# A dilated 7x7 convolution in front of a token attention: its sum over column taps taken from a pass through DRAM into TensorE, and the stages behind it moved by four slots

## The reference

```python
x0 = x
x = _gn(x)                                     # each channel of each image to mean 0, variance 1
y = conv_general_dilated(x, conv_w, strides 1, padding 15, rhs_dilation 5)   # 7x7, one output channel
y = batch norm of y
imp = sigmoid(gelu(y))                         # (B, 1, 110, 110)
xs = x * imp
idx = sort(top_k(imp, 192))                    # 192 pixels of each image
tokens = xs at idx + positions at idx          # (B, 192, 32)
t1 = layernorm(tokens + attention(tokens))     # 8 heads of 4
t2 = layernorm(t1 + feed forward of t1)
out = x0 + (x with t2 written at idx)
```

## Time and profile before

| | us |
|---|---|
| median of 3 runs | 1159.2 |
| lowest, highest | 1155.85, 1162.91 |
| span of the profiled execution | 1225.6 |
| TensorE busy in it | 971.3 (79%) |
| VectorE busy | 835.0 (68%) |
| ScalarE busy | 774.3 (63%) |
| GpSimd busy | 631.8 (52%) |
| mean granted TensorE clock | 0.884 |

### The profile page before, as it was taken

One profiled execution on the slowest core, in us unless ns is written; L12 is line 12 of the kernel. 1 busy time (PEld: TensorE's weight loads), 2 busy tenths in 40 slices (PEclk: granted clock), 3 DMA queues, 4 the chain that ended last, 5 costly groups with the idle time before them and its releaser, 6 DMA issues.

```text
span 1225.6 us, 21628 instructions
## 1 busy us (share of the span) xinstructions
PE 971.3 (79%) x6440; PEld 762.4 (62%) x6440; DVE 835.0 (68%) x2114; ACT 774.3 (63%) x1899; POOL 631.8 (52%) x851
## 2 busy tenths in 40 slices
PE   3986865689888988898889889986786786488676
PEld 2765643577667766776678667865664565366544
DVE  5345776488558967896879677976694676455644
ACT  2545644486547786877688768875866575267543
POOL 4333316632665368546854576557516655562352
PEclk8998988799879999999899999998987589699855
DMA  9998977555566989898989888965453555436778
GB/s 244 314 264 227 272 210 180 146 159 157 133 156 184 266 217 237 236 291 208 233 238 274 228 238 227 265 187 143 132 169 98 132 154 151 123 98 195 212 221 269
DMA packets 176252, 247.82 MB, mean 202 GB/s; under 512 B 65512, under 2 KB 71912, under 8 KB 176136
## 3 DMA queue, kind: packets, MB, share of 16 engines
q1 hardware_dynamic: 167944, 244.03, 71.9%
q0 software_dynamic: 8192, 2.40, 1.5%
HBM read 124.53 MB, written 121.80 MB: 201 GB/s over the span
## 4 chain that ended last, share of the span: by engine, by line
PE 38%; DVE 20%; ACT 12%; issue 9%; DMA 9%; another core or an unknown queue 6%; POOL 5%; SPq 1%; ACTq 0%; DVEq 0%; POOLq 0%
PE cv L527 10%; PE sc L646 7%; PE pp L659 4%; PE xb L511 4%; PE tr L561 3%; DVE res L1350 3%; ACT wgt L843 3%; PE ib L574 2%; ACT pr L872 2%; PE ms L675 2%; DMA table<-xt 2%; DMA X<-in_x 2%; DVE stats L1126 2%; DMA tok_pos<-in_pos,idx 2%
## 5 line engine op out<-in xcount | busy, mean ns | idle before, releaser
L527 PE MATMUL cv<-X,w_conv 128*128 128x330 f32 (+1 forms) x1024 | 302.2, 422 | 11.6 <-issue 5.9
L527 PEld LDWEIGHTS cv<-X,w_conv 128*128 128x128 f32 x1024 | 193.3, 203 | 45.9 <-issue 12.1
L843 ACT ACTIVATE wgt<-ib,eps_col,mom 128x440 f32<-128x440 f32 (+1 forms) x256 | 177.6, 701 | 46.3 <-DVE res L1350 22.0
L1145 DVE TENSOR_SCALAR_CACHE_REDUCE junk<-flat,th 128x379 bf16<-128x379 f32 x200 | 120.6, 603 | 115.3 <-ACT th L829 89.3
L511 PE MATMUL xb<-cst,X 128*110 128x128 f32 x900 | 153.7, 297 | 48.8 <-ACT xt L809 28.3
L646 PE MATMUL sc<-k_b,qm 128*128 128x192 f32 x768 | 172.2, 353 | 16.2 <-DVE pixf L1245 7.3
L1046 POOL TENSOR_SCALAR res<-res,mom 128x440 f32<-128x440 f32 (+1 forms) x152 | 96.0, 634 | 171.0 <-DVE res L1350 169.3
L1350 DVE SCALAR_TENSOR_TENSOR res<-tr,mom,wgt 128x440 f32<-128x440 f32 (+1 forms) x192 | 122.2, 641 | 71.4 <-PE tr L561 31.0
L809 ACT COPY xt<-xb 110x512 f32<-110x512 f32 x225 | 131.6, 585 | 58.9 <-PE xb L511 30.7
L872 ACT ACTIVATE pr<-sc,least 128x192 f32<-128x192 f32 x384 | 137.1, 415 | 31.0 <-DVE least L1314 18.6
L659 PE MATMUL pp<-cst,pr 128*96 128x128 f32 x768 | 122.5, 284 | 33.6 <-ACT pt L883 25.4
(11 more groups left out here) (170 smaller groups left out, 1534.2 us busy)
## 6 DMA issues: line engine op xcount, KB each, us to landing
table<-xt SPq DMA_DIRECT2D x240, 224.0 KB
rt<-table SPq DMA_DIRECT2D x240, 224.0 KB
out<-res SPq DMA_DIRECT2D x320, 137.5 KB
X<-in_x SPq DMA_DIRECT2D x64, 412.5 KB, 6.4
X<-in_x SPq DMA_DIRECT2D x64, 343.8 KB, 6.5
conv_rows<-cvr SPq DMA_DIRECT2D x64, 188.0 KB
y<-conv_rows SPq DMA_DIRECT2D x64, 165.4 KB
out<-res SPq DMA_DIRECT2D x64, 68.8 KB
```

Of the source, the lines that this page charges most:

```text
L527: last = mm(cv[:, 0:CUT[half]], w_conv[:, 4 * q + z], X[:, m % XI, at0:at0 + CUT[half]], start=z == 0, stop=z == 3)
L843: last = A(wgt[:, n % 2, at0:at0 + w], ib[:, at0:at0 + w], ACT.Identity, scale=mom[:, NB * g + b, 2:3], bias=eps_col[:, 1:2])
```

## The change

The convolution is turned around. Now `X` is the stationary operand and the weights are what streams: for each of the five rows inside a block (`r`), and each of six row-block groups (`k`), `conv_rows` loads 110 pixels of a row (four row blocks by 32 channels on the partitions) and streams 49, 70, 70, 70, 63 or 35 columns of weights, which are column tap by output row block. The result lies with pixel columns on 110 partitions. ACT copies it into `taps` in two parts (three rows, 462 columns, then two rows, 308 columns; `rows_copy`), each written 110 elements apart. `conv_taps` then multiplies each of the seven taps with a shifted identity (`shift`), so that the shift by 5 pixels and the sum over taps happen in PSUM, and ACT copies 110x110 into `yy` (`taps_copy`). `cvr`, `y7`, `conv_rows` in DRAM, `round_out`, `taps_in` and `importance_sum` are gone. `w_conv` shrinks from 1024 to 105 columns, `cst` grows by 140. Image `b` has its rows in slots BASE[b] to BASE[b]+4 and its taps in BASE[b]+5. All stages from GELU on have numbers smaller by 4; LOAD, INTO, MOMENTS and NORMAL stay.

```diff
-    OUT_T, CUT = 11, (3 * H, 2 * H)
+    KG, WIDE = 6, H // DIL * KS
+    SPLIT_R = 3
-        TAPS, SUM = (10, 17, 25, 31), (15, 20, 28, 32)
-        GELU, IMP_OUT, FLAT, SEARCH, IMP_IN = 33, 35, 38, 40, 58
...
-        SCATTER, BACK, IMPB = 122, 127, (123, 127, 135, 142)
+        TAPS = 5
+        GELU, IMP_OUT, FLAT, SEARCH, IMP_IN = 29, 31, 34, 36, 54
...
+        SCATTER, BACK, IMPB = 118, 123, (119, 123, 131, 138)
...
+        rows_at = {BASE[b] + r: (b, r) for b in range(NB) for r in range(DIL)}
+        taps_at = {BASE[b] + TAPS: b for b in range(NB)}
...
-                eng.wait_ge(conv_ok, upto(conv_ok, (m - XI) // NB, 4 * ((m - XI) % NB) + 3))
+                eng.wait_ge(conv_ok, upto(conv_ok, (m - XI) // NB, 2 * ((m - XI) % NB) + 1))
...
-            def round_out(g, r):
...
-            def taps_in(g, b):
...
-            def conv_part(g, r, first, last_z):
...
+            def conv_rows(g, b, r):
+                m = NB * g + b
+                if r == 0 and m:
+                    pe.wait_ge(y_cp, upto(y_cp, 0, m - 1))
+                if r == SPLIT_R:
+                    pe.wait_ge(cv_cp, upto(cv_cp, g, 2 * b))
+                at0 = WIDE * (r % SPLIT_R)
+                for k in range(KG):
+                    pe.wait_ge(xn_ok, upto(xn_ok, g, 3 * b + k // 2))
+                    low = 4 * k - KS // 2
+                    lo, hi = max(0, low), min(H // DIL, low + KS + 3)
+                    w0 = KS * (KS + 3) if k == KG - 1 else KS * (lo - low)
+                    row = H * (DIL * k + r)
+                    last = mm(cv[0:H, at0 + KS * lo:at0 + KS * hi], X[:, m % XI, row:row + H], w_conv[:, w0:w0 + KS * (hi - lo)],
+                              start=k == 0, stop=k == KG - 1, skip_group_check=True)
+                if r in (SPLIT_R - 1, DIL - 1):
                     last.then_inc(conv_ok, 1)
+            def conv_taps(g, b):
+                pe.wait_ge(cv_cp, upto(cv_cp, g, 2 * b + 1))
+                for k in range(KS):
+                    last = mm(cv[0:H, 0:H], taps[:, k], shift[:, DIL * k:DIL * k + H], start=k == 0, stop=k == KS - 1)
+                last.then_inc(y_ok, 1)
...
-            def round_copy(g, r):
...
+            def rows_copy(g, b, part):
+                act.wait_ge(conv_ok, upto(conv_ok, g, 2 * b + part))
+                lo, hi = ((0, SPLIT_R), (SPLIT_R, DIL))[part]
+                nc.scalar.copy(taps[:].rearrange("p k (q r) -> p r q k", r=DIL)[:, lo:hi],
+                               cv[0:H, 0:WIDE * (hi - lo)].rearrange("p (r q k) -> p r q k", r=hi - lo, k=KS)).then_inc(cv_cp, 1)
+            def taps_copy(g, b):
+                act.wait_ge(y_ok, upto(y_ok, g, b))
+                if g:
+                    act.wait_ge(imp_ok, upto(imp_ok, g - 1))
+                nc.scalar.copy(yy[:, b], cv[0:H, 0:H]).then_inc(y_cp, 1)
...
-            def importance_sum(g, b):
-                dve.wait_ge(y7_in[b], upto(y7_in[b], g))
-                v.reduce_sum(yy[:, b], y7[:, b].rearrange("p k j -> p j k"), AX).then_inc(y_ok, 1)
```

More of the change, by code:

```diff
@@ L83, in preact_conv_token_attention @@
         bones_f = take(128, 128)
+        shift = take(H, H + (KS - 1) * DIL)
         blk = sb("blk", [128, 128], fp16)
@@ L192, in preact_conv_token_attention @@
         xn_ok = raised("xn_ok", 3 * NB)
[L193 to L196, removed]
+        conv_ok = raised("conv_ok", 2 * NB)
+        cv_cp = raised("cv_cp", 2 * NB)
         y_ok = raised("y_ok", NB)
+        y_cp = raised("y_cp", NB)
         gelu_ok = raised("gelu_ok")
@@ L465, in _ @@
                     back_in(g, n + RT)
-                for g, n in at(s, 1, U):
-                    if n in round_end and round_end[n] % 2:
-                        round_out(g, round_end[n])
-                for b in range(NB):
-                    for g, n in at(s, TAPS[b]):
-                        taps_in(g, b)
                 for g, n in at(s, PARTS_OUT):
@@ L750, in _ @@
                 for g, n in at(s, 0, U):
-                    for part in rounds[n][0:1]:
-                        conv_part(g, part[0], part[1], part[2])
+                    if n in rows_at:
+                        conv_rows(g, *rows_at[n])
+                    if n in taps_at:
+                        conv_taps(g, taps_at[n])
                 for g, n in at(s, SCORES, U):
@@ L757, in _ @@
                     thresholds(g)
-                for g, n in at(s, 0, U):
-                    for part in rounds[n][1:2]:
-                        conv_part(g, part[0], part[1], part[2])
                 for g, n in at(s, RANKS):
@@ L1416, in _ @@
                     find_ranks(g)
-                for b in range(NB):
-                    for g, n in at(s, SUM[b]):
-                        importance_sum(g, b)
                 for g, n in at(s, GELU + 1):
@@ L1492, in positions, with conv_bands @@
     return pe
-def conv_bands(w, rows=11):
+def conv_bands(w):
     import numpy as np
     C, n, _ = w.shape
-    out = np.zeros((4 * C, 8, 128), np.float32)
-    for z in range(8):
-        half, at = z // 4, z // 4 * 2 + z % 4
-        for s in range(4):
-            low = 4 * at + s - rows * half - 3
-            for t in range(max(0, low), min(rows - 1, low + n - 1) + 1):
-                if 4 * at + s < 2 * rows:
-                    out[C * s:C * s + C, z, t:n * rows:rows] = w[:, :, t - low]
-    return out.reshape(4 * C, 8 * 128)
+    wide = n + 3
+    out = np.zeros((4, C, wide, n), np.float32)
+    for s in range(4):
+        for d in range(s, s + n):
+            out[s, :, d] = w[:, s - d + n - 1]
+    end = out[:, :, 0:wide // 2].copy()
+    end[2:] = 0
+    return np.concatenate([out.reshape(4 * C, -1), end.reshape(4 * C, -1)], axis=1)
 def packed_weights(a, C, NB, H, half):
```

98 lines of the change are left out of this document (26 added, 72 removed).

## The result

The changed kernel takes 1211.7 us (median of 4, 1208.7 to 1216.0) against 1158.8 (1155.9 to 1162.9): ratio 1.044 [1.041, 1.048]. The forecast was 1130 with a range of 1102 to 1161; it was wrong in sign.

What follows compares the result with a forecast made beforehand. The prediction took transfers to bound the first stretch and TensorE, with DVE and DMA close behind, the overlapped one. Its terms summed to -31 us on the profiled 1225.6, scaled -29, giving 1130 us, range 1102 to 1161.

Steps and rivals of the forecast that it cites:

- "If all, -12. I take 0": TensorE's convolution work, 237 to 225 us at full clock: between +35 and -12 us depending on the empty slots, taken as 0.
- products of 145 ns: Sign of being wrong: TensorE's new products taking 145 ns, as if load and stream didn't overlap, instead of about 95.
- "GpSimd: I take +4": Normalising on GpSimd: an image's first row now needs all three normalised parts, before one; +4 us.
- second rival: Slower: POOL's parts late behind gathers and scatters, 2.7 us twice in 8 groups, 43 us; 1167 us, chance 0.1.
- "-17" at the group's end: End of a group's convolution: DVE's tap wait and sum before Gelu replaced by taps and a copy; -17 us.
- "-6" for the other sums: The other 24 tap sums, 36.5 us off DVE: between 0 and 36 us, taken as -6.
- "-5" for transfers: Convolution data no longer written and read back, 22.6 MB: -5 us in the first stretch.
- "-5" for the slots: The end comes four slots sooner: between -14 and 0 us, taken as -5.
- "-4" for SP: SP's standing still at the convolution, 26.5 + 22.5 us, goes: -4 us.
- "+3" for strided copies: ScalarE's new copies write elements 440 bytes apart at 1.7 times the time per element: 0 to 15 us, taken as +3.
- first rival: Gain stays off the path: TensorE's unevenness, sums beside other work, strided copies; +7, 1166 us, half as bad 1148; chance 0.2.

Runs made afterwards that it cites:

- e_wide: Changed kernel with every row product streaming 105 columns instead of 35 to 70, importance not the reference's: 1180.6 us, 1.018 of the kernel before.
- e_norm: Changed kernel with an image's three normalising parts one slot sooner: 1187.2 us, 1.023 of the kernel before.
- e_sum1: Kernel before with each VectorE sum reading one tap of seven, importance not the reference's: 1154.1 us, 0.996 of the kernel before.
- e_pad_norm: Changed kernel streaming 105 columns per row product, surplus ones over zeros, and normalising one slot sooner: 1164.3 us, 1.004 of the kernel before.
- e_late4: Changed kernel with the stages from Gelu on put back by four slots to their old numbers: 1208.8 us, 1.041 of the kernel before.
- e_contig: Changed kernel with ScalarE writing `taps` in adjacent elements, tap products loading at 28-byte steps, five DMAs for `ge` instead of one: 1213.7 us, 1.048.
- e_even_dve2: e_dve2 with products of images 0 to 2 dealt 6, 6, 6, 4, 4, 4 over six slots, taps in the seventh: 1156.2 us, 0.996.
- e_dve2: e_pad_norm with image 2 of each group normalised by VectorE instead of GpSimd: 1161.2 us, 1.000 of the kernel before.

## Why the prediction was wrong, step by step

**"If all, -12. I take 0": the pace was right, the clock was left out.** This is the largest of the errors, 31 of 82 us; alone it would have brought the forecast level with the kernel before. The forecast multiplied 2368 products by their price at full clock. It worked out itself that the convolution moves from stream-bound to load-bound, and took for granted that TensorE would be granted the clock as before. It was not: 374 us at half clock in place of 235, and products every 186 ns there in place of 97. e_wide shows it by the one thing it changes: more columns streamed, the same loads, the same pace, the clock back to 0.892, -31 us. The list of signs that the forecast gave for being wrong held products of 145 ns, but no clock.

**"GpSimd: I take +4": right mechanism, wrong size.** The second rival said 2.7 us twice in each group, 43 us, and gave it one chance in ten on the ground that POOL would be about level. e_norm measured 25 us. Timed from one `xt` copy of ScalarE (L773, one in a slot) to the next, the slot in which image 2 starts took 6.9 us on average in the fifth to seventh group and 2.8 in e_norm; the slot of image 0's start took about 3 in both. The third to eighth group show this loss at image 2, 3.6 to 4.6 us each and 24 us together; the first two do not.

**"-17" at the group's end: the stall moved.** DVE's 20.7 us of waiting for the taps are gone. But, timed in the same way, the slot with the wait fell from 8.2 to 3.8 us while the new Gelu slot took 7.2, where the same place in the round had 4.4: net 1.6 us a group in the repeating stretch, 13 us in 8 groups at most. The forecast named the Gelu stage as what is late next and let it cost its 3 us; it had counted the taps' removal in full beside it.

**"-6" for the other sums:** with the group's end included, all 32 were worth some 5 us (e_sum1). The term was inside its bounds and near its size; together with the point above, the 23 us forecast for both were too many.

**"-5" for transfers, "-5" for the slots, "-4" for SP:** the ramp answers these together, with the first group's end and its sums in it. In e_pad_norm, with the clock given back, it is 18 us shorter than before (175.7 against 193.5), where the three terms were 14. e_late4 could not part the slots from the transfers by its time, and no run isolates what SP's 49 us were worth.

**"+3" for strided copies:** they took 972 and 703 ns against some 820 and 590 forecast. The forecast took 1.7 times per element beside a fixed 150 ns; against the adjacent writes of e_contig (540 and 417 ns) the same reckoning gives 2.1. Its effect on the end was not isolated: the only cure tried cost more than it saved.

**What took the rest.** In e_pad_norm the ramp's 18 us are lost again in the seven groups, 22 us or 3.2 a group. Waits of the kernel before, profiled again:
```profile
DVE tok L1288 <- DMA tok_pos<-in_pos,idx: 27.2, 6, 13.0
PE pp L614 <- DVE tok L1295: 22.3, 4, 14.6
```
Waits of e_pad_norm:
```profile
PE cv L488 <- POOL X L958: 7.2, 5, 3.8
PE pp L581 <- DVE tok L1265: 49.3, 8, 14.6
DVE tok L1258 <- DMA tok_pos<-in_pos,idx: 45.1, 8, 13.0
```
TensorE and DVE now stand and wait for the gathered tokens in every group. From the index (the line above) to VectorE's first use of the tokens a middle group takes 38.0 to 38.1 us where before it took 36.3 to 37.6 (on average 1.1 more), and TensorE reaches the place sooner, so part of what it saves ahead of it is spent waiting there. This was the first rival's kind of loss, at a place that it did not name. But over the seven groups the longer chain makes only some 9 of the 22 us. That it is not the whole the fastest version shows: in e_even_dve2 the chain takes 36.1 to 36.9 us in a middle group and is in no group longer than before, and the seven groups still take 788.5 us against 778.4. What lengthens the rest of a group, about 2 us in e_pad_norm, stays open.

**The sum again.** Forecast 1130; +31 for the clock; +21 for POOL above the 4 taken; that is 1182. The remaining 30 are gains not had. With both cures the ramp gives 18 us, more than the terms forecast for it, so they are missing in the seven groups, which take 22 us more than before where the terms for the group's end and the sums were to take some 20 off. The longer chain to the tokens is some 9 of the 22; these parts overlap, and no run divides them further.

## What to carry to other kernels

When a change replaces long streams by many short ones behind full-size loads, count the streamed columns beside the pace: here streaming 46 more columns in each product, at nearly equal pace, gave back 2.6% through the clock (e_wide), and zeros do as well as weights (e_pad_norm, clock 0.896). Before work is called free on an engine that is in order, list what each image or tile now needs first and what stands ahead of that on the queue; a first consumer that needs three parts where it needed one cost 25 us where 4 were forecast. And find the chain that the change does not shorten (here index to tokens, 36 to 41 us in a middle group), because savings ahead of it can arrive as waiting: e_norm took 19.5 us off one wait of TensorE and put 17.7 on another. Last, profile the kernel before more than once: one wait was 2.4 us in one execution and 25.4 in the next.

## What the runs showed of the hardware

- TensorE's busy time did not tell its clock. Between 30 and 108 us it was busy 69.74 of 78 us and granted 0.79; with the longer streams of e_wide 66.41 of 78, granted 0.96. The float32 products of both have the same loads.
- A stationary operand whose elements lie 28 bytes apart loads at about half speed: fourteen products of 110 columns in 2.82 us against 1.44. This load does not follow the clock: in e_contig the tap products come every 199 ns at either clock level, in after every 97 at the upper and 187 at the lower. ScalarE's copies into elements 440 bytes apart took 972 ns where adjacent ones took 540. The Trainium skill ("SBUF — State Buffer", "Door 1: The DMA port swizzle (why `[64,N]` ≈ `[32,N]`)") states a penalty for every access that crosses into a new 16-byte line; both pairs agree with it in kind, and it gives no figure for either.
- Streams hide behind loads: at full clock 12 products of 35 to 70 columns took 1.09 us and of 105 columns 1.15.
- How soon a gather's data can be used is not told by the pace of issue: in the middle groups the last of 24 took 3.6 to 3.7 us from its start to first use in e_pad_norm and 5.5 to 6.9 in after, both issued in 33.5 us, and 5.4 to 6.1 in e_dve2, issued in 30.6.
- Each Gelu or Exp waits for its table load: 1.28 us of load, and the activation starts 1.29 to 1.30 us after the load's start (ScalarE's timeline above).
